# Cross attention of both layers: the value product's waves are issued two at a time

## Chip, cores and metric

One core of a Trainium2 chip. The metric is the time of one execution on the device, in microseconds. The kernel is a whole network of two layers in one launch; the change concerns the cross attention, which stands once in each layer.

## What is computed

Each layer begins with cross attention from 512 rows (x, normalised) to 8192 rows of context, with 16 heads of 32 columns. Layer 0 has a mask over the 8192 keys, layer 1 has none. Everything else of the network (a state-space block, a linear attention, two mixtures of experts) is untouched.

```python
# layer 0 (layer 1: no mask, scale 32 ** -0.5, full projections)
energy = jnp.einsum('nqhd,nkhd->nhqk', q, k)              # 512 x 8192, per head
energy = jnp.where(mask == 0, jnp.float32(-1e+20), energy)
attention = jax.nn.softmax(energy / jnp.sqrt(jnp.float32(EMBED)), axis=3)
out = jnp.einsum('nhql,nlhd->nqhd', attention, v).reshape(n, q_len, EMBED)
return out @ Wo.T + bo
```

## The kernel before

A head is cut into 64 blocks of 128 keys by 512 queries, and two blocks make one of 32 steps (`PAIRS`). In each step the engines do this:

- TensorE: `scores(2g)` (L663, the matmul is L676), two matmuls `maxima` (L639, L651) that prepare the row maxima of the next head, `scores(2g+1)`, then what `waves_after` (L711) finds due. Scores use two PSUM banks in turn, so a score must wait until the exponential of the score two before has been taken. TensorE's instructions are issued in this order and stay in it.
- ScalarE: one exponential for each score (`exponentials`, L772; L776), from PSUM into a ring of 7 (layer 0) or 10 (layer 1) buffers of two blocks. The last two buffers are memory of `xnT`, so the trace calls them by that name.
- VectorE: the maximum over rows of the maxima's two banks (L834 in layer 0, L830 in layer 1), and in steps 3 to 6 an addition for the denominators (L860, L863).
- GpSimd and DMA: the rest of the denominators' additions (L951, L933, L937).
- SP: loads of keys (L607) and of the values in quarters of a head (L613), the latter when the waves that read the quarter before are done.

In layer 0 the mask is added by TensorE in front of the score (L675), except for every fourth block: there ScalarE writes the mask into the bank first (`mask_first`, L778; L781), after the exponential of the score that used this bank, and the score waits for that. This block is the first score of each odd step.

A **wave** (`wave`, L679; L694, and L690 for a sum) multiplies the values of up to four blocks with their exponentials. Each is a product with 32 output rows, and the four stand beside each other in the array's four groups of 32 columns. As the numbers are fp32, each matmul has two records in the trace, so a wave has eight, in two rounds of four. In layer 1, twelve waves of a head take three blocks and one sum for the denominators. There are 16 waves a head in layer 0 and 19 in layer 1. `Waves.step(w)` says behind which step a wave is issued: the first step by whose scores the last block of the wave has its exponential. Step 32 is step 0 of the next head. In layer 0 that is every even step; in layer 1 the steps 2, 4, ..., 12, then 14, 15, 17, 18, 20, 21, 23, 24, 26, 27, 29, 30 and 32.

Besides, `max_rows` (L655, L660) is issued in step 29, ScalarE takes the values over in step 1 (`take_values`, L787), and `head_out` (L699, L706 to L708) is issued in step 10 for the head before; ScalarE's `head_rows` (L792, L795) follow it. `step` is also read by `waves_after` and by ScalarE's condition for `take_values`; `last`, `done` and `quarter_done`, by which others wait for a wave, go by the wave's number and not by its step.

Of the kernel before, what the change touches and what calls it, by code (L numbers as in the profile page):

```python
# [51 lines left out]
class Kernel:  # L52


    def __init__(self, nc, ins, out, ctx):
        self.nc = nc
        self.i = ins
        self.out = out
        self.ctx = ctx
        self.live, self.old, self.cleared = [], [], []  # L60
        self.ntmp = 0
        self.ident = self.sbuf(ctx, "ident", [P, P], F32)
        self.ident_big = self.sbuf(ctx, "ident_big", [P, P], BF16)
        self.ones = self.sbuf(ctx, "ones", [P, P], F32)
        self.x = self.sbuf(ctx, "x", [P, TT, D], F32)
        self.xnT = self.sbuf(ctx, "xnT", [P, DT, T], F32)
        self.psum = ctx.enter_context(nc.psum_tensor("psum", [P, 8, 512], F32))
# [353 lines left out]
class Waves:  # L421


    def __init__(self, by_pe):
        self.values, self.sums = [], []
        self.to_sum = [2 * p + j for p in by_pe for j in range(2)]
        left, t = list(self.to_sum), 0
        while t < KT:
            with_sum = bool(left) and t >= left[0] // 2 * 2
            self.sums.append(left.pop(0) if with_sum else None)  # L430
            self.values.append(list(range(t, t + 3 if with_sum else t + 4)))
            t = self.values[-1][-1] + 1
        self.count = len(self.values)
# [4 lines left out]

    def step(self, w):

        return -(-(self.values[w][-1] + 1) // 2)

    def last(self, blocks):
        return max(w for w in range(self.count) if self.sums[w] in blocks or set(self.values[w]) & set(blocks))
# [91 lines left out]
def cross_attention(k, ctx, q_hi_lo, k_hi_lo, v_heads, wo, w_out, x_rows, comb, scale, masks, attT):  # L536
# [10 lines left out]
    if masked:  # L547
        sums = Sums([0, 1, 2, 3, 4], [], list(range(5, PAIRS - 2, 3)))
    else:
        sums = Sums([0, 1, 2, 3, 4], [12, 15, 18, 21, 24, 27], [7, 10, 13, 16, 19, 22, 25, 29])  # L550
    waves = Waves(sums.by_pe)
    q_stack = [k.sbuf(ctx, "q_stack", [QROWS + 2, T], F32R) for _ in range(n_q)]
    k_ring = k.sbuf(ctx, "k_ring", [QROWS + 2, kring, KC], F32R)
    v_buf = [k.x[:, j, :] for j in range(4)]
# [413 lines left out]
def l0_cross(k):  # L968
    x_rows = k.dram("x0_kept", [P, TT, D])
    with ExitStack() as outer:  # L970
        attT = k.sbuf(outer, "attT", [P, DT, T], F32)
        with ExitStack() as ctx:
            mask_k = k.sbuf(ctx, "mask_k", [P, KT, T], F8)
            comb = k.sbuf(ctx, "comb", [P, DH], F32)
            with ExitStack() as tmp:
# [6 lines left out]
                with k.nc.Block() as block:  # L982
# [14 lines left out]
                    def _(e):  # L997
# [3 lines left out]

            wo = mask_q[:, 0, 0:2 * DT * D].bitcast(F32).rearrange("p (c n) -> p c n", c=DT)
            cross_attention(k, ctx, q.dram, k.k0, k.i["ctx_heads"], wo,
                            k.i["L0_xattn_WoT"].rearrange("(k p) n -> p k n", p=P),
                            x_rows, comb[:], D ** -0.5, (mask_q, mask_k), attT)


def l1_cross(k):
    x_rows = k.dram("x_kept", [P, TT, D])
    with ExitStack() as outer:  # L1010
        attT = k.sbuf(outer, "attT", [P, DT, T], F32)
        wo = k.sbuf(outer, "w_out", [P, DT, D], F32)
        with ExitStack() as ctx:
            comb = k.sbuf(ctx, "comb", [P, DH], F32)
            with ExitStack() as tmp:
# [7 lines left out]
                with k.nc.Block() as block:  # L1023
# [34 lines left out]
                    def _(e):  # L1058
# [3 lines left out]
                        q.pe(e, lambda c: [(wq[:, d, c * P:(c + 1) * P], k.xnT[:, d, :]) for d in range(DT)])  # L1062
                k.block_over()
            cross_attention(k, ctx, q.dram, k.k1, k.v1, wo[:], k.i["L1_xattn_WoT"].rearrange("(k p) n -> p k n", p=P),
                            x_rows, comb[:], DH ** -0.5, None, attT)

# [211 lines left out]
def scan_states(k, u, zs, delta, du, bc, dcol, a, s_half):  # L1278
# [9 lines left out]
    with ExitStack() as tmp:  # L1288
# [16 lines left out]
        with nc.Block() as block:  # L1305
# [13 lines left out]
            @block.gpsimd  # L1319
            def _(e):  # L1320
                for step in range(GT * per):
                    m, g = divmod(step, per)
                    if step >= n_db:
                        e.wait_ge(s_sum, NH * (step - n_db + 1))
                    e.tensor_tensor(db[step % n_db][:], du[:, m, :].unsqueeze(1).to_broadcast([P, NH, T]),  # L1325
                                    bc[0][:, g * NH:(g + 1) * NH, :], ALU.mult).then_inc(s_db, 1)
# [1617 lines left out]
```

## Time and profile before

| | us |
|---|---|
| median of 3 runs | 4396.85 (4392.42 to 4407.57) |
| profiled execution | 4394.22 |
| its span, first to last instruction | 4392.5 |
| TensorE busy | 3877.4 (88%) |
| VectorE busy | 2997.9 (68%) |
| ScalarE busy | 2355.4 (54%) |
| GpSimd busy | 1695.3 (39%) |

The cross attention of layer 0 runs from about 484 to 1484 us of the span and that of layer 1 from about 2600 to 3572. The busy time of TensorE is modelled at the ends of its matmuls: rows of a timeline overlap, and the start of a row is what can be relied on.

### The profile page before, as it was taken

To read this page: it belongs to the slowest core of one execution; us is meant where nothing else is said; L and a number is where in the kernel's file an instruction comes from. 1 tells how busy PE (TensorE), PEld (TensorE's weight loads), DVE (VectorE), ACT (ScalarE), POOL (GpSimd) and SP (SyncE) were. 2 spreads that over 40 slices of the span, in tenths; PEclk is the share of its full clock that TensorE was granted. 3 is DMA by queue.
4 is the path that set the end of the run, shared out by engine and by line. 5 is a ranking of instruction groups with operands and counts; after the bars stand their busy time and mean duration, and the time that the engine had idled before them with its cause. 6 is when DMAs were issued, how large, how long until landed. Compare 5 with 4: busy or idle time off the path is not lost. (4 is left out here: it accounts for less than half of the span.)

```text
span 4392.5 us, 50969 instructions
## 1 busy us (share of the span) xinstructions
PE 3877.4 (88%) x17656; PEld 2209.3 (50%) x17656; DVE 2997.9 (68%) x3608; ACT 2355.4 (54%) x3611; POOL 1695.3 (39%) x1007
## 2 busy tenths in 40 slices
PE   7996899999999685668999779999999979769997
PEld 6884344444444261137788534444444425347885
DVE  4333877878787359954888667777777734477886
ACT  2221477777777533312777426666566641247775
POOL 0001487787778606510000126666556650000000
PEclk9997899999999878889999869999999999779998
DMA  9997566676666400021888646666666550407886
GB/s 317 329 339 263 168 155 156 154 155 149 154 152 145 120 5 10 0 80 41 331 323 325 239 127 154 154 144 152 139 153 151 122 132 1 107 31 295 323 327 242
DMA packets 301737, 753.52 MB, mean 172 GB/s; under 512 B 55854, under 2 KB 89390, under 8 KB 267946
## 3 DMA queue, kind: packets, MB, share of 16 engines
q1 hardware_dynamic: 245322, 562.03, 38.7%
q0 software_dynamic: 47456, 171.46, 19.5%
q10 hardware_dynamic: 8704, 16.78, 1.1%
q8 instruction: 142, 2.33, 0.2%
q14 instruction: 113, 0.93, 0.1%
HBM read 485.01 MB, written 99.42 MB: 133 GB/s over the span
## 5 line engine op out<-in xcount | busy, mean ns | idle before, releaser
L776 ACT ACTIVATE prob<-psum 128x512 f32<-128x512 f32 x1552 | 891.4, 595 | 437.1 <-PE psum L676 399.0
L951 POOL TENSOR_TENSOR den_pool<-den_pool,prob 128x1024 f32<-128x1024 f32 x372 | 938.8, 2524 | 228.6 <-DVE den_pool L863 196.8
L676 PE MATMUL psum<-q_stack,k_ring 98*128 98x512 f32 x2048 | 1006.1, 509 | 20.4 <-ACT prob L776 14.5
L651 PE MATMUL psum<-k_ring,q_stack 96*128 96x512 f32 x2048 | 693.1, 423 | 106.1 <-DVE row_max L834 36.4
L830 DVE TENSOR_REDUCE row_max<-psum 128x1 f32<-128x1024 f32 x512 | 616.0, 1220 | 243.7 <-PE psum L651 240.6
L834 DVE CUSTOM_DVE_ANT_0 psum<-psum,mask_q 128x1024 f32<-128x1024 f32 x512 | 627.1, 1233 | 202.9 <-PE psum L651 187.8
L676 PEld LDWEIGHTS psum<-q_stack,k_ring 98*128 98x128 f32 x2048 | 395.3, 194 | 621.8 <-ACT prob L776 272.4
L1928 DVE TENSOR_TENSOR weight_lo<-weight_raw,weight_hi 128x2048 fp32r<-128x2048 f32 x240 | 548.0, 2289 | 132.6 <-ACT weight_hi L1871 131.5
L694 PE MATMUL psum<-prob,x 128*32 128x512 f32 x3104 | 517.5, 613 | 0.9 <-ACT prob L776 0.9
L651 PEld LDWEIGHTS psum<-k_ring,q_stack 96*128 96x128 f32 x2048 | 395.2, 200 | 213.5 <-issue 84.5
L1871 ACT ACTIVATE weight_hi<-weight_raw 128x2048 fp32r<-128x2048 f32 x240 | 457.7, 1917 | 69.9 <-DMA weight_raw<-in_L_ffn_w 35.5
L776 ACT ACTIVATE xnT<-psum 128x512 f32<-128x512 f32 x496 | 288.5, 594 | 126.6 <-PE psum L676 117.4
L1784 POOL DMA_DIRECT2D y_slots<-xnT x30 | 16.4, 548 | 822.2 <-ACT xnT L1893 822.2
L951 POOL TENSOR_TENSOR den_pool<-den_pool,xnT 128x1024 f32<-128x1024 f32 x124 | 311.8, 2515 | 49.1 <-DVE den_pool L863 37.6
L675 PE MATMUL psum<-mask_k,ident_big 128*128 128x512 fp8e4 x768 | 300.7, 392 | 12.8 <-ACT prob L776 8.2
L1364 PE MATMUL psum<-dB_u,ident 128*128 128x512 f32 x256 | 156.1, 709 | 99.7 <-DVE dB_u L1339 99.6
L933 POOL DMA_DIRECT2D den_dma<-prob x180 | 156.4, 869 | 170.4 <-ACT prob L776 96.4
L1325 POOL TENSOR_TENSOR dB_u<-delta_u,B_all 128x2048 f32<-128x2048 f32 x32 | 144.2, 4514 | 197.1 <-POOLq L1207 109.8
L694 PE MATMUL psum<-xnT,x 128*32 128x512 f32 x992 | 201.0, 606 | 0.7 <-ACT prob L776 0.7
L103 PE MATMUL psum<-weight_hi,hidden_T_hi 128*128 128x512 f32 x480 | 195.9, 408 | 3.8 <-DVE weight_lo L1928 3.7
L103 PE MATMUL psum<-weight_hi,hidden_T_lo 128*128 128x512 f32 x480 | 188.8, 393 | 0.0
L103 PE MATMUL psum<-weight_lo,hidden_T_hi 128*128 128x512 f32 x480 | 187.3, 390 | 0.0
(428 smaller groups left out, 6351.0 us busy)
## 6 DMA issues: line engine op xcount, KB each, us to landing
weight_raw<-in_L_ffn_w SPq DMA_DIRECT2D x120, 1024.0 KB, 6.9
den_dma<-prob POOLq DMA_DIRECT2D x204, 512.0 KB, 5.0
k_ring<-k_hi SPq DMA_DIRECT2D x1024, 64.0 KB, 2.3
weight_raw<-in_L_ffn_Wu SPq DMA_DIRECT2D x60, 1024.0 KB, 7.2
weight_raw<-in_L_ffn_Wd SPq DMA_DIRECT2D x60, 1024.0 KB, 5.8
den_dma<-xnT POOLq DMA_DIRECT2D x68, 512.0 KB, 4.9
k_ring<-k_lo SPq DMA_DIRECT2D x512, 64.0 KB, 2.6
ctxT<-in_ctxT SPq DMA_DIRECT2D x16, 1024.0 KB, 9.6
```

Source lines behind the costliest of these rows:

```text
L103: ins = e.matmul(out, lhsT, rhs, start=start and n == 0, stop=stop and n == len(terms) - 1)
L651: ins = e.matmul(max_banks(q)[:, a * KC:(a + 1) * KC], q_stack[h % n_q][0:QROWS, i * P:(i + 1) * P], k_ring[0:QROWS, (n + a) % kring, :], ...
L675: e.matmul(k.bank(b % 2), k.ident_big[:], masks[1][:, t, :], start=True, stop=False)
L676: e.matmul(k.bank(b % 2), k_ring[:, n % kring, kt * P:(kt + 1) * P], q_stack[h % n_q][:], start=not masked, stop=True, skip_group_check=ma ...
L694: ins = e.matmul(vbank[n * DH:(n + 1) * DH, :], v_buf[t // 16][:, t % 16 * DH:(t % 16 + 1) * DH], prob[(PAIRS * h + t // 2) % n_p][:, t % ...
L776: e.activation(prob[b // 2 % n_p][:, b % 2, :], k.bank(b % 2), ACT.Exp, scale=scale).then_inc(s_exp, 1)
L830: e.reduce_max(out, max_banks(q), AXIS_X).then_inc(s_red, 1)
L834: e.tensor_tensor_reduce(out=max_banks(q), in0=max_banks(q), in1=masks[0][:, i, 2 * c2 * KC:2 * (c2 + 1) * KC], scale=1.0, scalar=-3.0e38, ...
L933: e.dma_start(den_dma[:], tile, accum_op=ALU.add).then_inc(s_ddma, 16)
L951: e.tensor_tensor(den[:], den[:], tile, ALU.add).then_inc(s_dpool, 1)
L1871: e.activation(hi[q % RING][:], raw[q % RAW][:], ACT.Copy).then_inc(s_whi, 1)
L1928: e.tensor_tensor(lo[q % RING][:], raw[q % RAW][:], hi[q % RING][:].bitcast(F32), ALU.subtract).then_inc(s_wlo, 1)
```

## The change

Waves w and w+1 (w even) are issued together, behind the step at which the later of the two was due. A last wave without a partner stays where it was.

```diff
 class Waves:
-    def __init__(self, by_pe):
-        self.values, self.sums = [], []
+    def __init__(self, by_pe, together):
+        self.values, self.sums, self.together = [], [], together
...
     def step(self, w):
-        return -(-(self.values[w][-1] + 1) // 2)
+        last = min(w - w % self.together + self.together, self.count) - 1
+        return -(-(self.values[last][-1] + 1) // 2)
...
-    waves = Waves(sums.by_pe)
+    waves = Waves(sums.by_pe, 2)
```

## Rows read from the trace of the kernel before

**Rows 1.** Stretches, one head of layer 0 and of layer 1: from:to, length, busy times

```profile
795.60:858.40 62.80, 62.23 (x319) 27.19 (x318) 47.60 (x73) 47.00 (x84) 50.15 (x29) 1.00 0.69 155
2907.50:2967.60 60.10, 58.26 (x294) 25.57 (x294) 45.38 (x41) 39.00 (x68) 34.86 (x21) 1.00 0.64 146
```

**Rows 2.** Timeline of TensorE, layer 0: start us, us, engine, line, operation

```profile
704.10 0.50 PE L676 MATMUL psum<-q_stack,k_ring 98*128 98x512 f32 x1
...
705.41 0.58 PE L676 MATMUL psum<-q_stack,k_ring 98*128 98x512 f32 x1
...
706.34 0.58 PE L676 MATMUL psum<-q_stack,k_ring 98*128 98x512 f32 x1
706.85 1.07 PE L694 MATMUL psum<-prob,x 128*32 128x512 f32 x8
707.85 0.50 PE L676 MATMUL psum<-q_stack,k_ring 98*128 98x512 f32 x1
```

**Rows 3.** Timeline of ScalarE, the same stretch

```profile
706.68 0.60 ACT L781 ACTIVATE psum<-mask_k 128x512 f32<-128x512 fp8e4 x1
```

**Rows 4.** Timeline of TensorE, layer 0, step 10: a wave and the head's output

```profile
816.02 1.06 PE L694 MATMUL psum<-prob,x 128*32 128x512 f32 x8
816.90 0.59 PE L706 MATMUL psum<-o_sb,comb 128*32 128x512 f32 x1
...
817.33 0.59 PE L706 MATMUL psum<-o_sb,comb 128*32 128x512 f32 x1
...
817.87 0.50 PE L676 MATMUL psum<-q_stack,k_ring 98*128 98x512 f32 x1
```

**Rows 5.** Timeline of TensorE, layer 0, head 0: first scores of steps 0 and 1

```profile
483.73 0.59 PE L676 MATMUL psum<-q_stack,k_ring 98*128 98x512 f32 x1
...
485.63 0.50 PE L676 MATMUL psum<-q_stack,k_ring 98*128 98x512 f32 x1
```

**Rows 6.** Timeline of ScalarE, layer 0, head 0, step 0

```profile
484.98 0.60 ACT L781 ACTIVATE psum<-mask_k 128x512 f32<-128x512 fp8e4 x1
```

**Rows 7.** Timeline of ScalarE, layer 0, steps 30 and 31

```profile
856.60 0.59 ACT L755 ACTIVATE q_stack<-psum 2x512 fp32r<-2x512 f32 x1
857.21 1.09 ACT L776 ACTIVATE prob<-psum 128x512 f32<-128x512 f32 x2
```

**Rows 8.** Timeline of TensorE, layer 1, two steps (PEld is the weight load)

```profile
3014.70 0.50 PE L676 MATMUL psum<-q_stack,k_ring 98*128 98x512 f32 x1
...
3015.89 0.19 PEld L676 LDWEIGHTS psum<-q_stack,k_ring 98*128 98x128 f32 x1 [0.42 <-ACT prob L776]
...
3018.03 0.50 PE L676 MATMUL psum<-q_stack,k_ring 98*128 98x512 f32 x1
```

**Rows 9.** Timeline of VectorE and TensorE, layer 1: steps 2, 3 and 8

```profile
2910.84 0.50 PE L676 MATMUL psum<-q_stack,k_ring 98*128 98x512 f32 x1
...
2913.23 0.50 PE L676 MATMUL psum<-q_stack,k_ring 98*128 98x512 f32 x1
...
2914.24 1.23 DVE L830 TENSOR_REDUCE row_max<-psum 128x1 f32<-128x1024 f32 x1 [1.19 <-PE psum L651]
...
2922.54 0.70 PE L651 MATMUL psum<-k_ring,q_stack 96*128 96x512 f32 x2 [0.97 <-DVE row_max L830]
```

**Rows 10.** Timeline of ScalarE, layer 1, step 2

```profile
2911.16 1.09 ACT L776 ACTIVATE prob<-psum 128x512 f32<-128x512 f32 x2
```

**Rows 11.** Stretches, scores (L676) alone, last head of each layer: TensorE busy (count)

```profile
1454.90:1467.93 13.03, 8.44 (x16) 3.15 (x16) 1.00 0.46 90
3547.50:3561.78 14.28, 7.37 (x18) 2.90 (x18) 1.00 0.56 109
```

**Rows 12.** A stretch of layer 1; after the five busy times the granted clock

```profile
2796.40:2799.80 3.40, 3.40 (x13) 1.04 (x12) 2.70 (x3) 0.80 (x2) 2.67 (x2) 0.50 0.07 19
```

**Rows 13.** Line 876, both layers: duration in ns, min/median/max

```profile
L876 DVE TENSOR_TENSOR attT<-attT,den_of_heads x26: 269/692/3041, 769.0 to 3591.0; 128x128 f32<-128x128 f32 x24, 128x512 f32<-128x512 f32 x2
```

## Prediction

> **What bounds the kernel now.** I read the table of stretches first, for one whole head of each layer [rows 1]. The masked layer (0) takes 62.8 us a head and TensorE is busy for 62.2 of them; layer 1 takes 60.1 with 58.3 busy. ScalarE has 47 and 39, VectorE 48 and 45. So TensorE's queue sets the pace, but its busy time hides short waits, and the question is what stands between its instructions. For that the timeline of one stretch is read by start times.
>
> Layer 0 [rows 2]. Call the four scores of two steps C, D (even step) and A, B (odd step). From the even step's first score C (705.41) to the next A (707.85) is 2.44 us; the odd step, A to C, is 1.31. Two steps are 3.75, with one wave of values in them, after D. That wave takes 1.00 (706.85 to 707.85). A is special: its mask is not added by TensorE but written into its bank by ScalarE (L781), and this copy must follow the exponential of C, which frees the bank. ScalarE starts the copy at 706.68 and takes 0.60 [rows 3]: it ends at 707.28, when the wave is in flight. The reader should see that TensorE doesn't wait for the copy only because the wave lies in front of A.
>
> **The change part by part.** It computes the same values with the same matmuls; it only moves half of the waves two steps later, behind another one. In layer 0 (16 waves a head) steps 2, 6, 10, ..., 30 lose their wave and steps 4, 8, ..., 28 and the next head's 0 have two. In layer 1 (19 waves: 18 in 9 pairs and one alone) the pairs stand at steps 4, 8, 12, 15, 18, 21, 24, 27, 30. No instruction is added, and no wait: the exponentials that a wave reads are behind the score in front of it either way. What a later wave holds up: its buffer of exponentials (7 in layer 0) is wanted again 7 steps after it was filled and is now released after 4 instead of 2, so ScalarE is not stopped; SP's load of a value quarter in layer 1 is released one step later and asked for two steps after that; the sums on GpSimd wait for exponentials, not for waves. I cost these at nothing; if one of them fell behind, it would show as ScalarE idle in front of L776 for something other than a score.
>
> *A step with a second wave.* No wave directly behind a wave stands in the trace, but the head's output does: three matmuls in the same column groups. The wave at 816.02 has two rounds, the output's rounds start at 816.90 and 817.33, the next score at 817.87 [rows 4]. So rounds follow at 0.43 to 0.44, and two more cost 0.86. The bound below is that; the bound above is a whole wave with its entry and exit, 1.00. I take 0.86, from the nearest row. Price of a double step in layer 0: 2.44 + 0.86 = 3.30.
>
> *An even step that loses its wave, layer 0.* TensorE alone would need 2.44 less the wave's 1.00. But A now waits for ScalarE's copy. Head 0 shows this: it has no wave in step 0, and there C starts at 483.73 and A at 485.63, which is 1.90 [rows 5]; the copy started at 484.98 and took 0.60 [rows 6], so it ended at 485.58, 0.05 before A. The same comes out of the steady stretch: C 705.41, end of copy 707.28, A at about 707.33, that is 1.92. The bounds are 1.87 (end of the copy) and 1.97; I take 1.91. The step gains 0.53, where its wave cost 1.00.
>
> So four steps of layer 0: before 2 x 3.75 = 7.50, after 3.30 + 1.31 + 1.91 + 1.31 = 7.83, or **0.33 longer**. The work of TensorE has shrunk, its wait has grown by more.
>
> *Steps that are not plain.* In step 10 the head's output follows; it takes the place in front of A that the wave had, so the two missing rounds are all gain: 816.02 to 816.90, 0.88. In step 30 ScalarE also turns the row maxima (856.60) before the two exponentials at 857.21 [rows 7]; these end near 858.3 whatever TensorE does, and the next head's first scores wait for them: of 0.53 only about 0.1 is left. Step 2 has ScalarE's take-over of the values just ahead: A starts some 0.06 later than elsewhere, gain 0.47. VectorE is no limit here: it needs 48 us of 63.
>
> Per head, layer 0: 8 x 0.86 = 6.88, less 5 x 0.53 + 0.88 + 0.1 + 0.47 = 4.10: +2.8. Fifteen heads: +42. The last head computes no maxima for a next one: eight steps take 13.03 [rows 11], 6.52 for four. With 1.91 for the step without a wave, 1.2 to 1.3 for the odd ones and 0.86 on the other it is 7.3: +0.8, eight times, +6. **Layer 0: +48 us.**
>
> *Layer 1.* There is no mask. A step without a wave takes 1.19 (3014.70 to 3015.89) and the wait that ends it is for an exponential [rows 8]; one with a wave 2.14 (3015.89 to 3018.03). So a wave taken out gives 0.95, and one put behind another costs 0.86: a pair of plain waves gains 0.09. That holds at steps 14/15, 17/18, 20/21, 23/24, 26/27 and 29/30: six times, -0.5. Step 10 loses its wave in front of the head's output (-0.88) and step 12 gets one (+0.86): 0. In steps 3 to 8 VectorE is the bound: from its first maximum (2914.24) to TensorE's in step 8 (2922.54) it works without a gap, 8.30, and TensorE idles 0.97 [rows 9]; no wave in that stretch counts. Before it, step 2 (2910.84 to 2913.23, 2.39) loses its wave; its first two exponentials run from 2911.16 to 2912.25 behind the take-over [rows 10], so it is 1.5: -0.9. Behind it, step 8 has the second wave: +0.86. Together 0. Per head -0.55, fifteen heads -8. In the last head nine steps take 14.28 [rows 11], 4.76 for three; a wave there costs less to have (TensorE has slack), so the second wave is dearer than what the other gives: about +0.4 six times, +2. **Layer 1: -6 us.**
>
> Sum: 48 - 6 = +42 on the profiled execution's 4394.2, so 4436; the median of the three runs is 2.6 above that execution. I forecast 4436, 0.9% slower.
>
> A rule that speaks against this: the Trainium skill, "TensorEngine Tiling (Array Packing)", Key Properties, says that changing the tiling mode drains TensorE. The change halves such switches. By this rule alone the kernel gets faster; its price is seen in rows 2 and 4 (exit from column groups 0.54, 817.33 to 817.87, against 0.43 between rounds), and it is in my sum already.
>
> **The rivals.**
> Faster, by fewer switches: if A did not wait, the step without a wave would be 2.44 - 1.00 and 0.11 less for the exit, 1.3, and four steps 3.30 + 1.31 + 1.3 + 1.31 = 7.2, 0.28 less than before: -36 in layer 0 and -6 in layer 1, 4352. For it: TensorE looks 99% busy. Against: the copy's end at 1.87 after C, in both stretches. This is the skill's rule above as a mechanism. Chance 0.09.
> No difference: the wait is there but small, because ScalarE comes out of the double wave with nothing behind; it decides at a step of 1.58 instead of 1.91. Against: the copy starts 1.25 to 1.27 after C with an idle ScalarE (head 0) and with a busy one. About 4392 to 4405. Chance 0.09.
> Slower still, by the clock: at 2796.4, behind the wait for VectorE in step 8 of another head of layer 1, the granted clock is 0.50 for 3.40 us [rows 12], which is 1.2 of 2.4 GHz. Three steps without a wave in a row, each ending in a wait for ScalarE, and then that wait are more idle time together than now. If twelve more heads fall once, each loses up to 1.7: +20, 4456. Chance 0.17. (The Trainium skill, "TensorE: Matmul & The Clock Gate", the section on psum-queue depth-cycling, tells of a kernel whose small idle gaps between groups made the clock go up and down; the row shows one fall only.)
>
> **How the numbers follow.** The forecast has 0.65. Its own range: a second wave at 1.00 instead of 0.86 would add 0.14 x 272 = 38; the step at 1.87 or 1.97 moves 4 either way; VectorE's divisions in heads 4, 8 and 12 took 0.27 to 3.04 us each [rows 13] with no pattern that I can foretell, some 6 either way. The upper end of the wave's cost is far from its row, so I give it a third of its weight: 4424 to 4452. With the clock's case the range is 4415 to 4462. A difference below 0.3% (13 us) can't be told from none here. Slower by more: 0.65 + 0.17 = 0.82; within: 0.09; faster: 0.09.
>
> **What would show it.** In the changed trace, layer 0: even steps with a pair of waves 3.3, those without 1.9, with TensorE's weight load of A waiting for L781, and a head of 65.6 instead of 62.8. Layer 1: 59.5 a head, steps of 1.19 and 3.0. Waves of a pair start 0.87 to 0.9 apart. I am wrong if steps without a wave are 1.3, if the second wave costs 1.0, or if a head of layer 1 grows; the last would point to the clock or to VectorE.

## The result and the profile after

The changed kernel takes 4456.46 us in the median of four runs (4449.27 to 4462.36) against 4397.35 in the same job: ratio 1.0135, 95% interval 1.0113 to 1.0156. It is slower by 59 us. The profiled execution took 4462.36, which is 68 more than the one of before and at the top of the four; all its stretches below add up to these 68 and not to 59. The line numbers of the cross attention are one higher than before.

First the stretches from the first to the last score of layer 0, of layer 1 and of layer 1's last head (scores alone; after the two busy times the granted clock, then DMA share and GB/s):

```profile
484.35:1527.92 1043.57, 550.59 (x1024) 203.15 (x1024) 1.00 0.64 143
2638.56:3634.12 995.56, 458.77 (x1024) 193.35 (x1023) 0.95 0.62 139
3564.45:3634.12 69.67, 30.91 (x64) 12.90 (x64) 0.76 0.41 89
```

and the same three of the kernel before:

```profile
483.72:1484.03 1000.31, 547.16 (x1024) 202.94 (x1024) 1.00 0.67 149
2599.95:3571.71 971.76, 458.03 (x1024) 191.81 (x1023) 0.98 0.63 142
3519.98:3571.71 51.73, 26.41 (x64) 10.47 (x64) 1.00 0.53 117
```

Layer 0 is 43.3 longer, layer 1 23.8, of which its last head alone has 17.9; what is left of the 68 (1.1) lies outside. The TensorE row of the page that shows the wait, before and after (for the scores of both layers; behind the second bar its idle time and what ended most of it):

```profile
L676 PE MATMUL psum<-q_stack,k_ring 98*128 98x512 f32 x2048 | 1006.1, 509 | 20.4 <-ACT prob L776 14.5
L677 PE MATMUL psum<-q_stack,k_ring 98*128 98x512 f32 x2048 | 1010.3, 511 | 71.2 <-ACT psum L782 50.0
```

One head of each layer, as in [rows 1]:

```profile
810.80:876.50 65.70, 61.95 (x319) 28.00 (x319) 49.04 (x73) 47.12 (x84) 50.95 (x29) 1.00 0.67 150
2946.80:3008.20 61.40, 59.27 (x294) 26.46 (x295) 47.26 (x41) 38.27 (x69) 37.48 (x23) 0.97 0.62 144
```

In layer 0 a head is 65.7 long instead of 62.8 and TensorE is busy for 0.3 less than before: by the profile's count all of the added time is idle. In layer 1 the granted clock of this head is 0.97, where it was 1.00.

**Layer 0.** Timeline of TensorE, a step with a pair of waves, its odd step, an even step without a wave and the next A; it answers to [rows 2]:

```profile
818.73 0.58 PE L677 MATMUL psum<-q_stack,k_ring 98*128 98x512 f32 x1
...
820.17 0.62 PE L695 MATMUL psum<-xnT,x 128*32 128x512 f32 x2
...
820.63 1.46 PE L695 MATMUL psum<-prob,x 128*32 128x512 f32 x10
822.02 0.50 PE L677 MATMUL psum<-q_stack,k_ring 98*128 98x512 f32 x1
...
823.35 0.58 PE L677 MATMUL psum<-q_stack,k_ring 98*128 98x512 f32 x1
...
825.27 0.50 PE L677 MATMUL psum<-q_stack,k_ring 98*128 98x512 f32 x1 [0.41 <-ACT psum L782]
```

Timeline of ScalarE, the copy of the mask in the step without a wave (compare [rows 3]):

```profile
824.62 0.60 ACT L782 ACTIVATE psum<-mask_k 128x512 f32<-128x512 fp8e4 x1
```

The step with two waves is 822.02 - 818.73 = 3.29, the odd step 1.33, the step without a wave 825.27 - 823.35 = 1.92. The two waves take 1.85 (820.17 to 822.02) where one took 1.00. In the step without a wave ScalarE's copy ends at 825.22 and the score A starts 0.05 later, with the copy named as what it waited for. In the whole of layer 0, 113 matmuls of TensorE name that wait, with 50.0 us together; before the change it was one, with 0.3, and none in a plain head. The rows of the weight load are no such sign. They name the copy in both kernels, with about the same idle time (the first is of A in [rows 2], where the copy had ended 0.57 before):

```profile
707.85 0.19 PEld L676 LDWEIGHTS psum<-q_stack,k_ring 98*128 98x128 f32 x1 [0.84 <-ACT psum L781]
825.27 0.19 PEld L677 LDWEIGHTS psum<-q_stack,k_ring 98*128 98x128 f32 x1 [0.83 <-ACT psum L782]
```

**Layer 1.** Timeline of TensorE in steps 7 and 8 of the same head (compare [rows 9]), and below it the stretch of the two waves; its clock is the last column but two:

```profile
2959.07 0.72 PE L677 MATMUL psum<-q_stack,k_ring 98*128 98x512 f32 x2
2960.86 0.70 PE L652 MATMUL psum<-k_ring,q_stack 96*128 96x512 f32 x2 [1.06 <-DVE row_max L831]
2961.40 0.40 PE L677 MATMUL psum<-q_stack,k_ring 98*128 98x512 f32 x1
2961.73 3.60 PE L695 MATMUL psum<-prob,x 128*32 128x512 f32 x16
2965.26 0.50 PE L677 MATMUL psum<-q_stack,k_ring 98*128 98x512 f32 x1
```

```profile
2961.70:2965.10 3.40, 3.40 (x17) 0.59 (x16) 2.41 (x3) 0.60 (x1) 2.95 (x2) 0.51 0.02 6
```

TensorE comes out of the wait for VectorE and the granted clock is at the lower of its two levels (1.2 of 2.4 GHz) for just the pair of waves: they take 3.53 instead of about 1.9. In heads where the clock stays, step 8 takes 4.27; here it takes 5.95. This happens in step 8 of 11 of the 15 heads before the last, before the change in 4 ([rows 12] is one of those; with a single wave such a head is 1.5 longer, with a pair about 1.7). In the last head there is no next head's maximum to compute, TensorE is idle more, and nine falls of the clock stand in it:

```profile
3586.65 0.73 PE L677 MATMUL psum<-q_stack,k_ring 98*128 98x512 f32 x2
3588.65 0.98 PE L677 MATMUL psum<-q_stack,k_ring 98*128 98x512 f32 x2 [1.26 <-ACT prob L777]
3589.56 1.75 PE L695 MATMUL psum<-xnT,x 128*32 128x512 f32 x8
3591.07 1.95 PE L695 MATMUL psum<-prob,x 128*32 128x512 f32 x8
3592.95 0.85 PE L677 MATMUL psum<-q_stack,k_ring 98*128 98x512 f32 x2
```

A pair of waves takes 3.39 here (3589.56 to 3592.95).

### The profile page after: what moved, and what is told of

It is laid out like the page before. It is cut to its first block and busy times, and to the rows that moved or that the text cites. A ratio compares the mean times of both kernels' runs of the same rounds, so it can differ in the third digit from the quotient of the medians.

```text
span 4460.6 us, 50969 instructions
## 1 busy us (share of the span) xinstructions
PE 3896.6 (87%) x17656; PEld 2246.2 (50%) x17656; DVE 3024.1 (68%) x3608; ACT 2344.8 (53%) x3611; POOL 1694.3 (38%) x1007
## 5 line engine op out<-in xcount | busy, mean ns | idle before, releaser
L695 PE MATMUL psum<-prob,x 128*32 128x512 f32 x3104 | 497.4, 632 | 0.9 <-ACT prob L777 0.9
L676 PE MATMUL psum<-mask_k,ident_big 128*128 128x512 fp8e4 x768 | 301.4, 392 | 16.6 <-ACT prob L777 11.5
L676 PEld LDWEIGHTS psum<-mask_k,ident_big 128*128 128x128 bf16 x768 | 74.8, 97 | 232.3 <-ACT prob L777 126.7
```

The lines of the kernel that those rows point to most:

```text
L676: e.matmul(k.bank(b % 2), k.ident_big[:], masks[1][:, t, :], start=True, stop=False)
L695: ins = e.matmul(vbank[n * DH:(n + 1) * DH, :], v_buf[t // 16][:, t % 16 * DH:(t % 16 + 1) * DH], prob[(PAIRS * h + t // 2) % n_p][:, t % ...
```

## The experiments

The theory has two halves. In layer 0 the wave hid ScalarE's copy of the mask; where the wave is gone the copy is exposed. In layer 1 the change is about neutral by itself, and the loss is the clock, which falls where TensorE waits. The rivals: bunched waves are dear by themselves; and the falls of the clock are only a symptom of something else.

**Which layer.** Each half of the change alone:

```diff
-    waves = Waves(sums.by_pe, 2)
+    waves = Waves(sums.by_pe, 2 if masked else 1)    # l0_pairs
+    waves = Waves(sums.by_pe, 1 if masked else 2)    # l1_pairs
```

> Pairs of waves in layer 0 alone; layer 1 issues each wave by itself, as before. Theory (exposed mask copies in layer 0, clock falls in layer 1): layer 0 takes 1043 to 1044 us from its first to its last score as in the changed kernel, +43, layer 1 972 as before; 4440. Rival (one cause for both layers, the bunched waves themselves, so that the cost goes by the number of pairs, 128 and 144): about half of the change's 59, 4425.

Measured: 4441.88 (ratio 1.0088, 1.0065 to 1.0110). Layer 0 alone, then layer 1, as above:

```profile
484.59:1530.15 1045.56, 551.04 (x1024) 203.22 (x1024) 1.00 0.64 143
2643.06:3613.53 970.47, 457.69 (x1024) 191.13 (x1023) 0.99 0.63 142
```

> Pairs of waves in layer 1 alone. Theory: layer 1 995 us, +24, layer 0 1000 as before, 4420; its granted clock falls to 0.50 in step 8 of most heads and in the double steps of the last head, though layer 0 is unchanged. Rival (bunched waves themselves, by number): 4428. Rival (the falls in layer 1 come from a shifted phase after a longer layer 0): layer 1 then loses the falls and takes 965, 4391.

Measured: 4409.89, but from 4398.64 to 4422.71 in ten runs (ratio 1.0017, 1.0007 to 1.0027), and the profiled one is the slowest of them:

```profile
484.11:1486.26 1002.15, 547.55 (x1024) 203.11 (x1024) 1.00 0.66 149
2603.52:3592.15 988.63, 458.12 (x1024) 192.56 (x1023) 0.96 0.61 140
```

Layer 0 has its own cost, +45, whatever layer 1 does. Layer 1 has +17 in this execution, with falls in step 8 of 12 of its heads, though layer 0 is as before; the falls are not a matter of a shifted start. By the medians layer 1 costs less than the two profiled executions show (+24 and +17): 7 us by this ratio, 11 by this median (4409.89 against 4398.80), and 15 between the changed kernel and `l0_pairs`. The expected 4420 is near the profiled execution and not near the median. The cost by number of pairs (128 and 144) would be about equal and is not. The last head here has three falls and takes 58.4, where it took 69.7 with nine: so their number differs between executions with the same layer 1. The ten runs spread over 24 us, and their mean granted clocks go with the times, from 0.932 in the fastest to 0.926 in the slowest.

**Layer 0 without the copy.** TensorE adds the mask for every block, once with single waves (control), once with pairs in layer 0:

```diff
-                if masked and b % 4 == 2:
-                    e.wait_ge(s_pre, b // 4 + 1)
-                elif b >= 2:
+                if b >= 2:
                     e.wait_ge(s_exp, b - 1)
-                if masked and b % 4 != 2:
+                if masked:
...
-                if masked and g % 2 == 0:
-                    mask_first(2 * g + 2)
```

> Control for the next: waves one at a time in both layers, but TensorE adds the mask for every block of layer 0 and ScalarE copies none. Every odd step has one more mask matmul, 0.23 less the 0.1 that the separate start of A cost: two steps 3.88 instead of 3.75, layer 0 +33 less what the ends of heads hide, 1030; in all 4428. All theories expect the same here.

> As nocopy_single, with pairs in layer 0 alone. Theory (the exposed copy is what makes pairs dear): without a copy the even step without a wave is 1.4, four steps 3.30 + 1.44 + 1.40 + 1.40 = 7.54 against 7.76, so pairs are now faster by 0.2 x 128 = 28: 4400. Rival (a second wave in a row costs more than it saves, whatever ScalarE does): slower than nocopy_single by 30 to 45, 4465.

Measured: single 4427.25 (ratio 1.0059, 1.0042 to 1.0076), pairs 4409.32 (1.0025, 1.0011 to 1.0038). Layer 0 of the two:

```profile
485.05:1513.79 1028.74, 568.70 (x1024) 206.79 (x1024) 1.00 0.65 145
```

```profile
484.07:1495.20 1011.13, 557.99 (x1024) 207.15 (x1024) 1.00 0.65 148
```

Timeline of TensorE with pairs, an even step without a wave and without a copy:

```profile
806.70 0.58 PE L675 MATMUL psum<-q_stack,k_ring 98*128 98x512 f32 x1
...
808.09 0.58 PE L675 MATMUL psum<-q_stack,k_ring 98*128 98x512 f32 x1
```

That step is 1.39 instead of 1.92, and now the pairs are faster than single waves, by 17.6 us in layer 0; a plain head takes 63.67 against 64.60. 28 were expected; the end of a head gives some back, step 31 has 1.86 instead of 1.40, and VectorE holds up step 8 a little. The sign of the same edit turns with the copy. So the saving of fewer switches between tilings is real, and it is the copy that outweighs it. The masks on TensorE cost more than they free, so this is no gain over the kernel before.

**The clock in the last head of layer 1.** To the changed kernel, two matmuls in each step where the other heads have their maxima, and, as the maxima run four steps ahead, in the last four steps of the head before; nothing reads them:

```diff
                 if g + PAIRS + LEAD < H * PAIRS:
                     maxima(g + PAIRS + LEAD)
+                elif not masked:
+                    fill_last()
...
+            def fill_last():
+                e.wait_ge(s_red, H * PAIRS)
+                for a in range(2):
+                    e.matmul(k.bank(2 + a), q_stack[(H - 1) % n_q][0:QROWS, 0:P], k_ring[0:QROWS, 0, :], start=True,
+                             stop=True)
```

> The changed kernel, and in the last head of layer 1 two extra matmuls in each step, at the place where the other heads have their maxima and of the same shape (q_stack by k_ring into a free bank); nothing reads them. Theory (the last head is long because TensorE, half idle, loses its clock): with more work in it the last head gets shorter, from 69.7 to about 58 (double steps 3.0 instead of 4.2), and no fall is left in it; heads 0 to 14 stay; about 4447. Rival (double waves wait for something else in the last head, with the clock a symptom): 70 or, with 56 more matmuls of 0.23, up to 80.

Measured: 4447.13 (ratio 1.0108, 1.0088 to 1.0128). The last head:

```profile
3557.01:3613.82 56.81, 28.11 (x64) 11.92 (x64) 1.00 0.47 103
```

More work, 12.9 us less time, and the granted clock is 1.00 instead of 0.76. The rival, that the clock is a symptom, falls. But 12.9 is the difference to the longest unfilled last head of all: over all traces with pairs in layer 1, an unfilled last head has 2, 3, 5 and 9 falls and takes 57.0, 58.4, 63.0 and 69.7, while the filled one has none in three traces and takes 56.8 to 56.9. In the whole time the gain of this filling is not clear of noise (1.0108 against 1.0135, the intervals overlap).

**The clock in step 8.** The same, and five more matmuls in step 8 of the other heads, ahead of the wait for VectorE:

```diff
+                if not masked and p == 8 and h + 1 < H:
+                    fill_wait(h, g)
...
+            def fill_wait(h, g):
+                if h >= 2:
+                    e.wait_ge(s_att, 2 * (h - 1))
+                for a in range(5):
+                    e.matmul(misc[0:2 * DH, :], q_stack[h % n_q][0:QROWS, 0:2 * DH],
+                             k_ring[0:QROWS, g // 2 % kring, :], start=True, stop=True, skip_group_check=True)
```

> The changed kernel with the extra matmuls of the last head and, in heads 0 to 14 of layer 1, five more in step 8 ahead of TensorE's wait for VectorE (64 output rows by 512, into rows of a bank that nobody holds then; nothing reads them). They take 1.1 of the 1.4 us that TensorE idles there. Theory (the clock falls for want of work in that wait): step 8 stays at 4.3 and its falls go, 1.65 each; layer 1 about 960, 4430. Rival (the falls come with the wait in step 8 but not for want of work, or the three steps without a wave before it are enough): steps of 5.9 stay in half of the heads or more, 4445.

Measured: 4432.02 (ratio 1.0073, 1.0056 to 1.0091). Step 8 of the same head as above, the stretch of its waves, and all of layer 1:

```profile
2953.97 1.32 PE L704 MATMUL psum<-k_ring,q_stack 96*64 96x512 f32 x5
2955.20 0.70 PE L652 MATMUL psum<-k_ring,q_stack 96*128 96x512 f32 x2
2955.73 0.40 PE L677 MATMUL psum<-q_stack,k_ring 98*128 98x512 f32 x1
2956.06 1.92 PE L695 MATMUL psum<-prob,x 128*32 128x512 f32 x16
2957.92 0.50 PE L677 MATMUL psum<-q_stack,k_ring 98*128 98x512 f32 x1
```

```profile
2955.20:2958.60 3.40, 3.40 (x23) 1.46 (x23) 3.25 (x3) 0.74 (x2) 2.26 (x1) 1.00 0.17 40
2642.15:3603.56 961.41, 454.30 (x1024) 192.18 (x1023) 0.99 0.63 144
```

The five matmuls (1.23 from the first to the maxima) lie in the time that TensorE waited anyway. None of the 15 heads has a fall in step 8 now; layer 1 is 34 shorter than in the changed kernel, 22 of it already in `fill_last` and 12 more here. The same maxima, the same wait for VectorE, the same three steps without a wave: only the idle time in the wait is gone.

**Where the wait comes from: two misses.** VectorE's additions in other steps, and one addition fewer:

```diff
-                if 3 <= p < 3 + sums.dve_adds:
-                    add_tile(h, p - 3)
+                if masked and 3 <= p < 3 + sums.dve_adds:
+                    add_tile(h, p - 3)
+                if not masked and p in (3, 5, 7, 9):         # spread_*
+                    add_tile(h, (p - 3) // 2)
...
-        sums = Sums([0, 1, 2, 3, 4], [12, 15, 18, 21, 24, 27], [7, 10, 13, 16, 19, 22, 25, 29])
+        sums = Sums([0, 1, 2, 3], [12, 15, 18, 21, 24, 27], [4, 7, 10, 13, 16, 19, 22, 25, 29])   # fewer_*
```

> The changed kernel with VectorE's four additions of layer 1 in steps 3, 5, 7, 9 instead of 3, 4, 5, 6, so that TensorE no longer waits for a maximum in step 8. Theory (falls of the clock follow that wait): no falls in heads 0 to 14 of layer 1, step 8 is 3.0 instead of 4.27 or 5.95, these heads 58.3, the last 62 to 70, layer 1 940; about 4405. Rival (falls come from three steps in a row without a wave): the falls stay with 1.7 each, layer 1 960, 4425.

> The kernel before with the same spread additions in layer 1. Step 8 is 2.14 instead of 3.32, and the six falls of the clock in layer 1 are fewer: heads 58.9, layer 1 936 to 945, about 4365. If the additions only move VectorE's bound to a later step, 4395.

Measured: 4451.13 (ratio 1.0122, 1.0103 to 1.0141) with pairs, 4402.48 (1.0013, 1.0003 to 1.0022) with single waves. Expected were 4405 and 4365, some 40 us less in both. Step 8 did get shorter. With single waves it takes 2.2 in all heads, and no fall is left in it. With pairs it takes 3.8 to 3.9 in nine heads, in eight of which TensorE waits 0.6 there (0.7 in the ninth), and these have no fall, though the three steps without a wave are still there. Five of the other six still have one (5.7 to 6.5), in three of them behind a wait of 0.84 to 0.86 and in one behind 0.56. So a shorter wait goes with fewer falls, but it does not rule them out. And an addition of VectorE now meets one of GpSimd. Timelines of VectorE and GpSimd in such a head with single waves:

```profile
2668.93 3.25 DVE L861 TENSOR_TENSOR den_pool<-prob 128x1024 f32<-128x1024 f32 x1
```

```profile
2668.37 6.01 POOL L954 TENSOR_TENSOR den_pool<-den_pool,prob 128x1024 f32<-128x1024 f32 x2
```

VectorE's takes 3.25 instead of 1.22, and with single waves TensorE waits 1.4 to 1.7 in step 6 of five heads instead of in step 8, in four of them with a fall behind it. (The Trainium skill, "GPSIMD Engine Reference", Specifications, says that GpSimd shares its SBUF interfaces with VectorE and contends with its instructions of two SBUF inputs; the rows fit.)

> The changed kernel with three of VectorE's additions a head in layer 1 instead of four; the fourth tile's sum goes by DMA. The wait in step 8 is shorter by 1.14 or gone. Theory (the falls of the clock in heads 0 to 14 follow the long wait in step 8, not the three steps without a wave before it): step 8 is 3.0 to 3.2 and has no fall; heads of layer 1 58.3 to 59, layer 1 945 to 955, about 4420. Rival (the row of steps without a wave is enough): falls stay, steps of 4.7, 4435.

> The kernel before with the same three additions. Step 8 is 2.14 to 2.25 instead of 3.32 and has none of the four falls that stand there: heads 59.0, layer 1 950, 4375 to 4380. If the DMA's sum comes later than VectorE's and holds up the head's output or GpSimd, the gain is lost elsewhere: 4395.

Measured: 4444.54 (ratio 1.0094, 1.0071 to 1.0117) and 4396.56 (0.9997, 0.9984 to 1.0009). Step 8 stayed at 4.27 and 3.32: the maximum that TensorE waits for stands behind three additions in VectorE's queue, and the fourth, which I took away, behind it. The expectation misread the queue. As repetitions with an unchanged wait they say that falls in step 8 come and go: 8 of 15 heads with pairs, 3 with single waves. But they are more frequent with pairs: over all traces with the waits as they were, 7, 8, 11 and 12 of 15 heads have one with pairs in layer 1, and 3, 3, 4, 4 and 5 with single waves.

**Towards a better kernel.** Pairs in layer 0 with a copy only behind a pair, and the spread additions:

```diff
-    waves = Waves(sums.by_pe, 2)
+    waves = Waves(sums.by_pe, 2 if masked else 1)
...
-                if masked and b % 4 == 2:
-                    e.wait_ge(s_pre, b // 4 + 1)
+                if masked and b % 8 == 2:
+                    e.wait_ge(s_pre, b // 8 + 1)
...
-                if masked and b % 4 != 2:
+                if masked and b % 8 != 2:
                     e.matmul(k.bank(b % 2), k.ident_big[:], masks[1][:, t, :], start=True, stop=False)
...
-                if masked and g % 2 == 0:
+                if masked and g % 4 == 0:
                     mask_first(2 * g + 2)
```

> Pairs in layer 0 alone, with ScalarE's copy of the mask only for the block behind a pair of waves (TensorE adds the mask for the others), and the spread additions in layer 1. Layer 0: 3.30 + 1.31 + 1.40 + 1.40 = 7.41 for four steps, 0.09 less than before, but the end of a head loses 0.5 (step 31 of 1.86 in the kernel without copies): 999 to 1003, no gain over single waves. Layer 1 as in the kernel with spread additions and single waves. So 4365 again; if pairs pay at all where no copy is exposed, a few us below it.

Measured: 4402.59 (ratio 1.0008, 0.9998 to 1.0018). A plain head of layer 0 takes 62.75 against 62.79: with the exposed copies gone the loss of 2.9 a head is gone too, and no more than that. The gain expected of layer 1 failed with the spread additions.

The other half: pairs in layer 1 alone, with both fillings:

> The same filling, but pairs of waves in layer 1 alone, layer 0 as before the change. If the falls were all that stood against pairs in layer 1, a head there is 59.5 against 60.1, without falls: layer 1 958 to 962 against 972, layer 0 1000 to 1002, 4383 to 4388, a little faster than before. If the filler doesn't stop the falls: 4400.

Measured: 4392.73 in twelve runs (4381.45 to 4396.94), ratio 0.9980, 0.9969 to 0.9990, where 4383 to 4388 was expected. The profiled execution, 4396.83, is close to the top of them:

```profile
484.49:1489.69 1005.20, 548.37 (x1024) 203.26 (x1024) 0.99 0.66 148
2605.19:3568.05 962.86, 454.37 (x1024) 191.68 (x1023) 0.99 0.63 144
```

It beats both kernels, by 0.2% the one before. A head of layer 1 without a disturbance takes 59.5 against 60.1, the last head 56.9 against 51.7, which is -4 for the layer; the rest of its -9 fits the falls in step 8 that the kernel before has (four heads, 1.5 each) and that are gone, all but one that begins in step 7 of head 1 and reaches into step 8 (5.55). The filling with single waves was not run, so how much of the 0.2% is due to the pairs stays open.

## Why the prediction was right and where it was wrong

Right was the whole of layer 0. Forecast were 3.30, 1.31, 1.91, 1.31 for four steps; the trace has 3.29, 1.33, 1.92, 1.31. A plain head was to get 2.8 longer and got 2.9 (62.79 to 65.70); the last one 6 and got 6.3. The named cause, A behind ScalarE's copy, is shown by the rows of after and by the pair of kernels without the copy, where the sign turns. The sign that I had named for it, a weight load of A that waits for the copy, stands in the kernel before as well and shows nothing; the matmul's own row does. The sum was 48, the trace has 43.3: missing from it is a gain that I had only put into the range. VectorE held up TensorE around its divisions in heads 8 and 12 before (66.75 and 65.76 for these heads), and in the longer head it doesn't (65.69 and 65.67): 7 less. "VectorE is no limit here" was wrong for these heads, and in head 8 the wait has a fall of the clock behind it; the stretch below is that of the fall, and step 25 in it takes 2.42 instead of 1.31.

```profile
1033.49 0.70 PE L651 MATMUL psum<-k_ring,q_stack 96*128 96x512 f32 x2 [1.56 <-DVE row_max L834]
1035.20:1038.50 3.30, 3.30 (x15) 1.41 (x7) 2.34 (x6) 0.69 (x2) 2.46 (x2) 0.50 0.83 159
```

Right were also the prices of layer 1's steps: 1.19 and 2.99, a pair gains 0.09, a head 0.55; heads without a fall take 59.51 against 60.12. **The step that failed is the sum of layer 1, "-6".** It took the granted clock as it was before. The trace has +24: about -9 for the pairs (0.6 a head), +13 for heads with a fall in step 8 (11 at about 1.7 against 4 at 1.5), +18 in the last head, and 2 from the rest. By the medians it is +7 to +15. A plain head grew from 60.1 to 61.4, which the prediction names as a sign that it is wrong and that points to the clock or to VectorE. The third rival had the place, the price (up to 1.7 each) and the time (4456 for a measured 4456.5), with a chance of 0.17. That the time fits is luck: it counted twelve more heads with a fall where the trace has seven, and it did not have the last head. There my sum had +2, from the scores' starts, and I did not ask what a head with less work for TensorE does to the clock. Slower was right either way, since layer 0 decides it. The median lies in the range of 4415 to 4462, but 20 us above the forecast and outside the narrower range of the likeliest case.

The two rivals on the other side fell. Fewer switches do save: a second wave costs 0.85 (820.17 to 822.02 is 1.85) where a separate one costs 1.00, which agrees with the rows of the head's output [rows 4], and pairs gain 17.6 in layer 0 when nothing hides behind a wave. That was in the sum. It is much less than what the step without a wave loses to the copy: 1.92 where that rival counted with 1.3 and the rival of no difference with 1.58. (The Trainium skill, "TensorEngine Tiling (Array Packing)", Key Properties: a change of tiling mode drains TensorE. The runs agree in direction.)

## What to carry to other kernels

Before you bunch work on the engine that looks full, list what the other engines do behind each piece of it: the piece that you move may be the cover of a copy, and the time shows up as a wait that no matmul's row of the old profile had. An engine that is 99% busy in the profile's count can still lose 4% to one such wait. A schedule with the same work and longer idle gaps can lose TensorE's clock for the burst behind the gap, and the burst is then just where it hurts; look at the granted clock behind each wait, and at the last round of a loop, where part of the work is missing.

## What the runs showed of the hardware

- The granted clock fell to 0.5 for 3.4 us behind waits of 1.0 to 1.3 us, in some heads of an execution and not in others with the same wait (1.06 in step 8 of head 5, with a fall, and of head 11, without one). With a pair of waves behind the wait a fall cost about 1.65 us in its step, with a single wave about 1.0. Five matmuls whose results nobody reads, in the idle time, kept the clock at 1.00 there in 15 of 15 heads of one trace and 14 of 15 of another, and the layer was 12 us faster (973.07 to 961.41, one trace each, both with the last head filled). (The Trainium skill, "TensorE: Matmul & The Clock Gate", the section on psum-queue depth-cycling, describes small idle gaps that make the clock go up and down; these runs show it with a count.)
- Rounds of matmuls into the four column groups follow each other at 0.43 us (0.45 after the first), whether or not they belong to one wave; from the last round to the next score it is 0.53 to 0.54.
- An addition of VectorE took 3.25 instead of 1.22 us beside one of GpSimd.
